# A graph network's gathers: GpSimd's rests wait for three tiles of a quad, with the fourth on a semaphore of its own

## The chip, the cores and the metric

The kernel runs on one core of one Trainium2 chip. The metric is the device time of one execution in microseconds: the median of the runs shown.

## The reference

Four graph networks follow each other on 3125 nodes of 128 features and 50000 edges that are sorted by their destination. After each, its output is added to its input and the sum is normalised over the features. What matters here is that every layer gathers a row of a node table for every edge, by the edge's source, and adds the results up by destination:

```python
def _layer(h, src, dst, e_w, w_neigh, w_root, b_root, g, b):      # network 0, three layers
    msg = e_w[:, None] * h[src]
    agg = jax.ops.segment_sum(msg, dst, num_segments=N)
    sum_w = jnp.clip(jax.ops.segment_sum(e_w, dst, num_segments=N), 1.0, None)
    out = agg / sum_w[:, None]
    out = out @ w_neigh.T + h @ w_root.T + b_root
    ...
# network 1: an edge network on edge_attr, joined with x[row], one layer
combined = jnp.concatenate([x[row], ef], axis=1)
msg = jax.nn.relu(combined @ Wn1 + bn1) @ Wn2 + bn2
out = jax.ops.segment_sum(msg, col, num_segments=x.shape[0])
# network 2: two layers with a table row for each source and edge type (8 types)
msg = xt[src, etypes]
agg = jax.ops.segment_sum(msg, dst, num_segments=x.shape[0])
# network 3: two attention layers; keys and values gathered by source and edge type (32 types)
kw = kT[src, :, etype]
m = vT[src, :, etype]
a = jnp.einsum('ehd,ehd->eh', kw, q[dst]) * pri[:, etype].T / SQRT_D
att = edge_softmax(a, dst, n)
```

## The kernel before

**Tiles, quads and steps.** The edges stand in 391 tiles of 128 (`EDGE_TILES`), four tiles to a quad, 98 quads (`TILE_QUADS`), the last with three tiles. A block of 128 nodes gets its sum by matmuls of a one-hot matrix (edge by node in the block) with the gathered rows, added up in PSUM. A tile whose edges reach over the end of a block is used twice, so the consumers go through 416 steps, 104 step quads, and look up in tables (`slot_i`, `blk_i`, `need_i`) which tile, which block and how many quads a step needs.

**Eight gather passes.** In each, `gathers` (L466) issues on GpSimd one indirect DMA for each tile (L479). It fetches 128 rows by the indices in `idx_s` into a ring of 60 tiles (`RING`) in SBUF. The passes, in order of time: 1 to 3 are the layers of network 0 (`aggregate_phase`, L683), of which 2 and 3 are the edge passes, in which `EdgeShare` also computes half of network 1's edge network on TensorE, ScalarE and VectorE and stores it; 4 is the block at L1182, which adds the stored edge part (`joins`); 5 and 6 are `aggregate_phase` for network 2; 7 and 8 are `score_phase` (L1874) of network 3, whose rows are 256 wide and in which SyncE also stores four tiles of values a step quad. Between the passes stand phases on the nodes, and every pass ends with a barrier of all engines.

**What orders the gathers.** The order is written out by hand. Four gathers of a quad go to one of 16 semaphores, `gathered[k % 16]`, 16 counts each. `hand_over(k)` (L470) waits for 64 counts more on that semaphore and raises `arrived` by one. VectorE waits for `arrived` in `release_steps` (L542) and passes `step_ready` on to TensorE; in pass 4 VectorE and in passes 7 and 8 VectorE and SyncE wait for it directly. From tile 60 on, GpSimd waits before each quad in `freed` for the step quad that last used the slots (`quad_done`, in other passes `mixed`), counted for the worst place of the block borders: at tile 60 it asks for step 28, so 32 tiles are in between; later in a pass this grows.

**The rests.** After the fourth tile of a quad, the loop below L480 hands over all quads but the newest, so that GpSimd waits for nothing that is in flight. Only where the number of quads is a multiple of `rest` does it hand over the newest too, and so waits until the gather that it issued last has landed. This is a rest. `rest` is 2 in the edge passes and 4 in the others.

```python
if t % 4 == 3:
    done = t // 4 + 1
    for k in range(handed[0], done if done % rest == 0 else done - 1):
        hand_over(k)
        handed[0] = k + 1
```

In an edge pass nothing is left over between rests, so both quads are handed over at the rest. After the loop the last two quads are handed over.

Of the kernel before, what the change touches and what calls it, by code (L numbers as in the profile page):

```python
# [17 lines left out]
H = 128  # L18
# [6 lines left out]
U = 16  # L25
# [7 lines left out]
EDGE_TILES = -(-E // P)  # L33
# [63 lines left out]
def build(nc, A, out):  # L97
    ctx = ExitStack()
    with ctx:
        def sb(name, shape, dt=F32):  # L100
            return ctx.enter_context(nc.sbuf_tensor(name, shape, dt))

        def signal(name):
            return Signal(ctx.enter_context(nc.semaphore(name)))

        def dram(name, shape, dt=F32):
            return nc.dram_tensor(name, shape, dt, kind="Internal").ap()


        table = dram("table", [NP, H])  # L110
        table8 = dram("table8", [NP * R8, H])
        table32 = dram("table32", [TABLE_NODES * T32, 2 * H])
# [27 lines left out]
        idx_s = sb("idx_s", [P, STEPS], I32)  # L140
# [39 lines left out]
        fetched = signal("fetched")  # L180
        go = signal("go")
        gathered = [signal(f"gathered{u}") for u in range(U)]
        arrived = signal("arrived")
        onehot_ready = signal("onehot_ready")
        step_ready = signal("step_ready")
# [280 lines left out]
        def gathers(pool, tab, width, freed, joins=None, rest=4):  # L466

            handed = [0]

            def hand_over(k):  # L470

                pool.wait_ge(gathered[k % U].sem, gathered[k % U].at(64 * (k // U) + 16 * min(4, EDGE_TILES - 4 * k)))
                if joins is not None:
                    joins(pool, k)
                pool.sem_inc(arrived.sem, 1)
            for t in range(EDGE_TILES):
                if t % 4 == 0 and t >= RING:
                    freed(pool, (t - RING + 3 + NB - 1) // 4)
                pool.indirect_dma_start(ring[:, ds(t % RING * 2 * H, width)], None, tab,  # L479
                                        bass.IndirectOffsetOnAxis(ap=idx_s[:, t:t + 1], axis=0)).then_inc(gathered[t // 4 % U].sem, 16)  # L480
                if t % 4 == 3:
                    done = t // 4 + 1
                    for k in range(handed[0], done if done % rest == 0 else done - 1):
                        hand_over(k)
                        handed[0] = k + 1
            for k in range(handed[0], TILE_QUADS):
                hand_over(k)

# [60 lines left out]
        def quad_pass_over():  # L549
            onehot_ready.base += ALL_QUADS  # L550
            quad_done.base += ALL_QUADS

        def gather_pass_over():
            quad_pass_over()
            arrived.base += TILE_QUADS
            for k in range(TILE_QUADS):
                gathered[k % U].base += 16 * min(4, EDGE_TILES - 4 * k)

        def fill_rows(pe, row):

# [122 lines left out]
        def aggregate_phase(tab, weight, root=None, row=None, sums=None, edges=None, ahead=None):  # L683


            with nc.Block() as block:
                @block.gpsimd
                def _(pool):
                    if ahead:
                        ahead.gpsimd(pool)  # L690

                    def freed(pool, n):
                        pool.wait_ge(quad_done.sem, quad_done.at(n + 1))
                    gathers(pool, tab, H, freed, rest=2 if edges else 4)

                @block.vector
                def _(dve):
# [80 lines left out]
                if edges:  # L778
# [5 lines left out]
                    def _(act):  # L784
                        edges.activations(act)
            gather_pass_over()
            step_ready.base += ALL_QUADS
            if sums:
# [389 lines left out]
        if STAGE >= 2:  # L1178
# [3 lines left out]
            with nc.Block() as block:  # L1182
                @block.gpsimd
                def _(pool):
                    def freed(pool, n):
                        pool.wait_ge(mixed.sem, mixed.at(n + 1))

                    def joins(pool, k):
                        pool.wait_ge(ring_in[k % HALF].sem, ring_in[k % HALF].at(16 * (k // HALF + 1)))
                    gathers(pool, table, H, freed, joins, rest=4)  # L1190

                @block.sync
                def _(sp):
# [43 lines left out]
                def _(pe):  # L1237
# [21 lines left out]
                    trips(pe, body)  # L1259
                    add_totals(pe)  # L1260
            gather_pass_over()
            totals_over()
            mixed.base += ALL_QUADS
# [340 lines left out]
        if STAGE >= 4:  # L1604
# [269 lines left out]
            def score_phase():  # L1874
# [4 lines left out]
                with nc.Block() as block:  # L1879
                    @block.gpsimd  # L1880
                    def _(pool):
                        stored_quads = [-1]

                        def freed(pool, n):
                            pool.wait_ge(mixed.sem, mixed.at(n + 1))
                            for m in range(stored_quads[0] + 1, n + 1):
                                pool.wait_ge(ring_out[m % QUADS].sem, ring_out[m % QUADS].at(64 * (m // QUADS + 1)))
                            stored_quads[0] = n
                        gathers(pool, table32, 2 * H, freed, rest=4)

                    @block.sync
                    def _(sp):
# [77 lines left out]
                onehot_ready.base += ALL_QUADS  # L1970
                arrived.base += TILE_QUADS
                for q in range(TILE_QUADS):
                    gathered[q % U].base += 16 * min(4, EDGE_TILES - 4 * q)
                for s in row_in:
                    s.base += 16 * TRIPS
                for s in (mixed, made, copied):
# [181 lines left out]
            for l in range(2):  # L2158
# [44 lines left out]
                by_type_phase(None, kvq_weights[l], sorted_kvq, layer=l)  # L2203
                key_value_table_phase(columns=l == 0)
                score_phase()
                softmax_phase()
                message_phase()
# [187 lines left out]
```

## Time and profile before

| | |
|---|---|
| median of 3 runs | 6471.04 us (6457.61 to 6473.24) |
| the profiled execution, its own time | 6410.16 us |
| its span | 6408.1 us |
| GpSimd busy | 3221.9 us (50%), of it the 3128 gathers 3001.8 us |
| TensorE busy, matmuls | 3293.9 us (51%) |
| VectorE, ScalarE busy | 2162.9 us (34%), 1006.4 us (16%) |

A share of busy time is an average over all stages. A gather on GpSimd is busy while its descriptors are written; the transfer lands later and isn't seen as busy time. A gap on GpSimd is shown in brackets ahead of the instruction that ended it, with what released it where the profile can tell; "issue" says only that it can't.

### The profile page before, as it was taken

The page shows a single profiled execution, that of the slowest core. Times are in us where ns is not written, and L with a number is a line of the kernel's source. Part 1 is how long each engine was busy: PE and PEld are TensorE (multiplying, and loading weights), DVE is VectorE, ACT ScalarE, POOL GpSimd, SP SyncE. Part 2 cuts the span into 40 slices and gives each one's busy share as a digit, 9 for nine tenths or more (in the row PEclk, how much of TensorE's full clock was granted, in tenths as well). Part 3 has the DMA queues.
Part 4 walks back from the last instruction along what each step waited for, and adds up shares of the span by engine and source line. Part 5 has one row for each costly group of instructions (what it writes and reads, how often), then busy time and mean ns, then how long its engine had stood idle before and what let it go on. Part 6 is the DMA issues. An engine that isn't in the chain of part 4 may idle for free. (4 is left out here: it accounts for less than half of the span.)

```text
span 6408.1 us, 51881 instructions
## 1 busy us (share of the span) xinstructions
PE 3293.9 (51%) x13857; PEld 2295.6 (36%) x13857; DVE 2162.9 (34%) x5075; ACT 1006.4 (16%) x2209; POOL 3221.9 (50%) x3406
## 2 busy tenths in 40 slices
PE   5554677767774555643463344643324356333263
PEld 3333455545552333332343232233324322333153
DVE  3222322232224222411121114533338544333485
ACT  0000322232222111200010002400004324000063
POOL 4665466546663666366646663046650320566403
PEclk7676777677776777755565556755557677555586
DMA  2111334333432332211131116976653579766453
GB/s 61 46 47 40 88 98 101 98 82 99 101 99 79 91 90 82 107 46 47 46 131 47 46 46 251 427 239 185 182 149 111 149 287 427 204 187 184 118 148 95
DMA packets 630965, 826.34 MB, mean 129 GB/s; under 512 B 93075, under 2 KB 510341, under 8 KB 618133
## 3 DMA queue, kind: packets, MB, share of 16 engines
q1 hardware_dynamic: 480117, 492.37, 22.9%
q0 software_dynamic: 120608, 276.12, 16.2%
q10 hardware_dynamic: 29952, 54.54, 2.9%
q8 instruction: 116, 1.90, 0.1%
q14 instruction: 172, 1.41, 0.1%
HBM read 470.63 MB, written 352.04 MB: 128 GB/s over the span
## 5 line engine op out<-in xcount | busy, mean ns | idle before, releaser
L479 POOL DMA_INDIRECT arena<-table,idx_s x3128 | 3001.8, 960 | 2353.5 <-issue 1095.5
L751 PE MATMUL ps<-arena,work 128*128 x4160 | 985.9, 378 | 1050.0 <-issue 934.9
L751 PEld LDWEIGHTS ps<-arena,work 128*128 128x128 f32 x4160 | 824.8, 274 | 1317.4 <-issue 1170.3
L1965 PE MATMUL ps<-arena,work 128*128 x1664 | 412.7, 426 | 693.7 <-issue 488.2
L1965 PEld LDWEIGHTS ps<-arena,work 128*128 128x128 f32 x1664 | 359.1, 317 | 748.6 <-issue 530.1
L459 DVE TENSOR_SCALAR work<-iota_row,dl_s,w_s 128x128 f32<-128x128 f32 x1248 | 350.4, 358 | 454.6 <-issue 349.4
L455 DVE TENSOR_TENSOR work<-ps,dl_s 128x512 f32<-128x512 f32 x208 | 143.8, 692 | 926.5 <-issue 617.0
L1934 DVE TENSOR_TENSOR arena<-arena,ps 128x128 f32<-128x128 f32 x832 | 182.7, 281 | 741.9 <-issue 500.0
L929 DVE SCALAR_TENSOR_TENSOR arena<-ps,vecs,arena 128x256 f32<-128x256 f32 x208 | 100.6, 484 | 893.9 <-issue 435.9
L1832 PE MATMUL ps<-arena,work 32*128 32x512 f32 x1600 | 299.1, 876 | 97.5 <-DVE work L1859 44.2
L510 PE MATMUL ps<-work,picks 128*104 128x512 f32 x416 | 313.4, 842 | 46.2 <-issue 42.8
L1863 DVE COPY arena<-ps 128x1024 f32<-128x1024 f32 x200 | 238.6, 1221 | 271.0 <-DMA table<-arena 164.8
L1254 PE MATMUL ps<-work,arena 128*128 128x128 f32 x832 | 173.5, 373 | 248.6 <-ACT arena L1232 153.7
L1654 POOL DMA_INDIRECT sorted_x<-work,pos_i x50 | 48.6, 973 | 479.8 <-DVE work L1747 465.2
L1254 PEld LDWEIGHTS ps<-work,arena 128*128 128x128 f32 x832 | 148.4, 267 | 382.4 <-ACT arena L1232 231.5
L863 PE MATMUL ps<-arena 128*128 128x128 f32 x832 | 212.3, 400 | 83.9 <-DVE arena L929 41.7
L1850 ACT ACTIVATE arena<-ps 128x1024 f32<-128x1024 f32 x200 | 198.1, 1022 | 309.7 <-DMA table<-arena 187.0
L1216 DVE TENSOR_TENSOR arena<-arena 128x128 f32 x416 | 94.7, 288 | 414.3 <-issue 245.1
L2145 PE MATMUL ps<-arena,onehot 128*128 128x128 f32 x1664 | 209.4, 280 | 21.7 <-DVE arena L2125 17.0
L863 PEld LDWEIGHTS ps<-arena 128*128 128x128 f32 x832 | 164.8, 278 | 123.0 <-DVE arena L929 64.2
L857 PE MATMUL ps<-arena 128*128 128x256 f32 x416 | 193.3, 560 | 28.9 <-ACT arena L897 25.0
L2145 PEld LDWEIGHTS ps<-arena,onehot 128*128 128x128 f32 x1664 | 194.7, 191 | 36.2 <-issue 30.7
(331 smaller groups left out, 3539.5 us busy)
## 6 DMA issues: line engine op xcount, KB each, us to landing
table<-arena SPq DMA_DIRECT2D x96, 2048.0 KB
onehot<-col_rows ACTq DMA_DIRECT2D x208, 256.0 KB
values<-arena SPq DMA_DIRECT2D x832, 64.0 KB
arena<-values SPq DMA_DIRECT2D x208, 256.0 KB
arena<-table,idx_s POOLq DMA_INDIRECT x3128
arena<-edge_times SPq DMA_DIRECT2D x208, 128.0 KB
edge_part<-arena SPq DMA_DIRECT2D x208, 128.0 KB
table<-arena SPq DMA_DIRECT2D x50, 512.0 KB
```

Of the source, the lines that this page charges most:

```text
L459: is_dst = dve.tensor_scalar(home[:, at + c, :], iota, dl_s[:, ds(j + c, 1)], weight[:, ds(j + c, 1)], ALU.is_equal, ALU.mult)
L479: pool.indirect_dma_start(ring[:, ds(t % RING * 2 * H, width)], None, tab, bass.IndirectOffsetOnAxis(ap=idx_s[:, t:t + 1], axis=0)).then_i ...
L510: mm = pe.matmul(quad_sums, picks[:, ALL_QUADS - n:2 * ALL_QUADS - n], deep[:, 4 * (n % DEEP):4 * (n % DEEP) + 4, :].rearrange("p c e -> p ...
L751: mm = pe.matmul(accf[:, ds(b, P)], o, arena[:, ds(slot, H)], start=False, stop=False, skip_group_check=True)
L857: pe.matmul(self.half_b, self.We2, self.hid[:, r, :], start=True, stop=True, skip_group_check=True).then_inc(turned.sem, 1)
L863: mm = pe.matmul(self.half_a[:, c * P:(c + 1) * P], self.ef[:, r, c * P:(c + 1) * P], self.Wn1b, start=True, stop=True, skip_group_check=True)
L1254: mm = pe.matmul(accf[:, ds(b, P)], relu_h[:, (i * U + u) % (4 * RELUS), :], o, start=False, stop=False, skip_group_check=True)
L1832: mm = pe.matmul(ps[:, 4 * kv + g, :], (value_ring if kv else key_ring)[rows, b % 2, :], (pair_v if kv else pair_k)[rows, half * 16:(half ...
L1850: act.activation(rows32[:, m % 3, :, kv * H:kv * H + 64].rearrange("p t (g c) -> p g t c", g=2), ps[:, 4 * kv:4 * kv + 2, :].rearrange("p ...
L1863: dve.tensor_copy(rows32[:, m % 3, :, kv * H + 64:(kv + 1) * H].rearrange("p t (g c) -> p g t c", g=2), ps[:, 4 * kv + 2:4 * kv + 4, :].re ...
L1965: mm = pe.matmul(ps[:, n % 8, c * P:(c + 1) * P], across_ring[:, n % DEEP, c * P:(c + 1) * P], Qn_flat[:, ds(b, P)], start=True, stop=True)
L2145: mm = pe.matmul(accf[:, ds(b, P)], o, msgs[:, 4 * q + c, :], start=False, stop=False, skip_group_check=True)
```

## The change

Of each quad only the first three tiles count on `gathered[k % 16]`, 48 counts a quad; the fourth counts on a new semaphore `fourth[k % 16]`. `hand_over(k)` waits for both. After the fourth tile of quad k is issued, quad k - 1 is always handed over, and never quad k. A rest is now a wait for the 48 counts of quad k alone, so for its first three tiles, while the fourth is in flight, and it stands behind the hand-over of quad k - 1. `rest` becomes 1 in the edge passes and 2 in the others. The loop ends with k = 96, so an edge pass has 97 rests and another pass has 48. The sums of the semaphores after a pass are changed to match.

```diff
+        fourth = [signal(f"fourth{u}") for u in range(U)]
...
-                pool.wait_ge(gathered[k % U].sem, gathered[k % U].at(64 * (k // U) + 16 * min(4, EDGE_TILES - 4 * k)))
+                pool.wait_ge(gathered[k % U].sem, gathered[k % U].at(48 * (k // U) + 16 * min(3, EDGE_TILES - 4 * k)))
+                if 4 * k + 3 < EDGE_TILES:
+                    pool.wait_ge(fourth[k % U].sem, fourth[k % U].at(16 * (k // U) + 16))
...
-                                        bass.IndirectOffsetOnAxis(ap=idx_s[:, t:t + 1], axis=0)).then_inc(gathered[t // 4 % U].sem, 16)
+                                        bass.IndirectOffsetOnAxis(ap=idx_s[:, t:t + 1], axis=0)).then_inc((fourth if t % 4 == 3 else gathered)[t // 4 % U].sem, 16)
                 if t % 4 == 3:
-                    done = t // 4 + 1
-                    for k in range(handed[0], done if done % rest == 0 else done - 1):
-                        hand_over(k)
-                        handed[0] = k + 1
+                    k = t // 4
+                    if k > 0:
+                        hand_over(k - 1)
+                        handed[0] = k
+                    if (k + 1) % rest == 0:
+                        pool.wait_ge(gathered[k % U].sem, gathered[k % U].at(48 * (k // U) + 48))
...
-                    gathers(pool, tab, H, freed, rest=2 if edges else 4)
+                    gathers(pool, tab, H, freed, rest=1 if edges else 2)
...
-                    gathers(pool, table, H, freed, joins, rest=4)
+                    gathers(pool, table, H, freed, joins, rest=2)
...
-                        gathers(pool, table32, 2 * H, freed, rest=4)
+                        gathers(pool, table32, 2 * H, freed, rest=2)
```

GpSimd's instructions at the start of the first pass (`rest` 4, then 2), with the semaphores that each waits for. A number behind x is a run of gathers without a wait, and a wait stands in the row of the gather behind it. Before:

```order
L479 DMA arena<-table,idx_s 128x128 x8
L479 DMA arena<-table,idx_s 128x128 [waits gathered0]
L479 DMA arena<-table,idx_s 128x128 x3
L479 DMA arena<-table,idx_s 128x128 [waits gathered1]
L479 DMA arena<-table,idx_s 128x128 x3
L479 DMA arena<-table,idx_s 128x128 [waits gathered2,gathered3]
L479 DMA arena<-table,idx_s 128x128 x7
L479 DMA arena<-table,idx_s 128x128 [waits gathered4]
```

Now:

```order
L482 DMA arena<-table,idx_s 128x128 x8
L482 DMA arena<-table,idx_s 128x128 [waits gathered0,fourth0,gathered1]
L482 DMA arena<-table,idx_s 128x128 x3
L482 DMA arena<-table,idx_s 128x128 [waits gathered1,fourth1]
L482 DMA arena<-table,idx_s 128x128 x3
L482 DMA arena<-table,idx_s 128x128 [waits gathered2,fourth2,gathered3]
L482 DMA arena<-table,idx_s 128x128 x3
L482 DMA arena<-table,idx_s 128x128 [waits gathered3,fourth3]
```

Before, the row with gathered2 and gathered3 is the rest behind 16 gathers. Now the row with gathered1 behind 8 gathers, and the one with gathered3 behind 16, are rests that leave the fourth tile out.

GpSimd's instructions at the start of the second edge pass (`rest` 2, then 1). Before:

```order
L479 DMA arena<-table,idx_s 128x128 x8
L479 DMA arena<-table,idx_s 128x128 [waits gathered0,gathered1]
L479 DMA arena<-table,idx_s 128x128 x7
L479 DMA arena<-table,idx_s 128x128 [waits gathered2,gathered3]
L479 DMA arena<-table,idx_s 128x128 x7
```

Now:

```order
L482 DMA arena<-table,idx_s 128x128 x4
L482 DMA arena<-table,idx_s 128x128 [waits gathered0]
L482 DMA arena<-table,idx_s 128x128 x3
L482 DMA arena<-table,idx_s 128x128 [waits gathered0,fourth0,gathered1]
L482 DMA arena<-table,idx_s 128x128 x3
L482 DMA arena<-table,idx_s 128x128 [waits gathered1,fourth1,gathered2]
L482 DMA arena<-table,idx_s 128x128 x3
```

A wait stood behind every second quad; now one stands behind each, and what it hands over is the quad before. Nothing moves on the other engines.

## Rows read from the trace of the kernel before

**Rows 1.** The page: span, busy time of each engine, and the gathers' group.
```profile
span 6408.1 us, 51881 instructions
PE 3293.9 (51%) x13857; PEld 2295.6 (36%) x13857; DVE 2162.9 (34%) x5075; ACT 1006.4 (16%) x2209; POOL 3221.9 (50%) x3406
...
L479 POOL DMA_INDIRECT arena<-table,idx_s x3128 | 3001.8, 960 | 2353.5 <-issue 1095.5
```

**Rows 2.** Windows of the eight passes, line L479 alone.
```profile
core 0: us, POOL busy (x), PEclk, DMA share, GB/s
63.95:617.42 553.47, 370.21 (x391) 0.65 0.18 47
672.80:1271.96 599.16, 371.44 (x391) 0.71 0.39 99
...
2000.03:2566.79 566.76, 394.17 (x391) 0.72 0.32 91
2652.31:3211.35 559.04, 377.30 (x391) 0.55 0.18 46
3276.95:3829.38 552.43, 370.49 (x391) 0.54 0.19 51
4206.91:4778.12 571.21, 373.68 (x391) 0.52 0.65 183
5465.61:6037.76 572.15, 372.85 (x391) 0.52 0.66 184
sum 4574.11, POOL 3001.83; mean POOL 375.23
```

**Rows 3.** Timeline, GpSimd, pass 1: start, length, instruction, [idle before].
```profile
82.87 0.95 POOL L479 DMA_INDIRECT arena<-table,idx_s  x1 [0.30 <-issue]
86.22 0.95 POOL L479 DMA_INDIRECT arena<-table,idx_s  x1 [2.41 <-issue]
87.47 0.95 POOL L479 DMA_INDIRECT arena<-table,idx_s  x1 [0.30 <-issue]
```

**Rows 4.** Timeline of all engines around a rest of the first edge pass.
```profile
1002.79 0.95 POOL L479 DMA_INDIRECT arena<-table,idx_s  x1 [0.30 <-issue]
1004.88 0.47 ACT L908 ACTIVATE arena<-ps,vecs 128x256 f32<-128x256 f32 x1 [5.54 <-remote]
...
1005.38 0.48 DVE L929 SCALAR_TENSOR_TENSOR arena<-ps,vecs,arena 128x256 f32<-128x256 f32 x1 [6.21 <-issue]
...
1006.00 0.95 POOL L479 DMA_INDIRECT arena<-table,idx_s  x1 [2.27 <-DMA arena<-table,idx_s]
...
1006.94 1.06 PE L751 MATMUL ps<-arena,work 128*128 x4
...
1010.55 0.48 DVE L929 SCALAR_TENSOR_TENSOR arena<-ps,vecs,arena 128x256 f32<-128x256 f32 x1 [3.55 <-issue]
```

**Rows 5.** Timeline, GpSimd: a long edge rest, then score rests of passes 7 and 8.
```profile
771.38 0.95 POOL L479 DMA_INDIRECT arena<-table,idx_s  x1 [3.25 <-DMA arena<-table,idx_s]
...
4326.24 0.95 POOL L479 DMA_INDIRECT arena<-table,idx_s  x1 [4.48 <-DMA arena<-table,idx_s]
...
5534.70 0.95 POOL L479 DMA_INDIRECT arena<-table,idx_s  x1 [2.58 <-issue]
```

**Rows 6.** Timeline, GpSimd, first edge pass: a pause behind a rest.
```profile
1018.08 0.95 POOL L479 DMA_INDIRECT arena<-table,idx_s  x1 [2.37 <-issue]
1019.97 0.95 POOL L479 DMA_INDIRECT arena<-table,idx_s  x1 [0.94 <-issue]
```

**Rows 7.** Timeline, TensorE beside GpSimd: pass 1, its end, the end of pass 6.
```profile
145.71 0.37 PE L751 MATMUL ps<-arena,work 128*128 x1 [2.44 <-issue]
...
147.11 0.29 PEld L751 LDWEIGHTS ps<-arena,work 128*128 128x128 f32 x1 [2.52 <-issue]
...
148.50 0.37 PE L751 MATMUL ps<-arena,work 128*128 x1 [2.42 <-issue]
...
161.18 0.95 POOL L479 DMA_INDIRECT arena<-table,idx_s  x1 [0.30 <-issue]
...
165.34 1.00 PE L751 MATMUL ps<-arena,work 128*128 x3 [0.34 <-issue]
...
165.62 0.94 POOL L479 DMA_INDIRECT arena<-table,idx_s  x1 [3.49 <-remote]
...
620.08 1.45 PE L751 MATMUL ps<-arena,work 128*128 x6 [1.73 <-issue]
...
634.07 1.05 PE L751 MATMUL ps<-arena,work 128*128 x8
...
3831.71 0.37 PE L751 MATMUL ps<-arena,work 128*128 x1 [0.33 <-issue]
3832.43 6.82 PE L751 MATMUL ps<-arena,work 128*128 x42 [0.34 <-issue]
```

More of the change, by code:

```diff
@@ L556, in gather_pass_over @@
             for k in range(TILE_QUADS):
-                gathered[k % U].base += 16 * min(4, EDGE_TILES - 4 * k)
+                gathered[k % U].base += 16 * min(3, EDGE_TILES - 4 * k)
+                fourth[k % U].base += 16 * (4 * k + 3 < EDGE_TILES)
         def fill_rows(pe, row):
@@ L1972, in score_phase @@
                 for q in range(TILE_QUADS):
-                    gathered[q % U].base += 16 * min(4, EDGE_TILES - 4 * q)
+                    gathered[q % U].base += 16 * min(3, EDGE_TILES - 4 * q)
+                    fourth[q % U].base += 16 * (4 * q + 3 < EDGE_TILES)
                 for s in row_in:
```

## The prediction

> **What bounds the kernel now.** I read the page first, then the windows of the eight gather passes, then the timeline of GpSimd inside them, and last TensorE beside it.
>
> The page: one core, 6408.1 us, no engine over 51% busy [rows 1]. The group of gathers, L479, holds 3001.8 of GpSimd's 3221.9 us, and its idle time names mostly "issue", that is, nothing that the view can name. The windows [rows 2] tell more: eight stretches of 391 gathers each fill 4574 us of the 6408. In each, GpSimd is busy for some 370 us of 552 to 600; the rest is gaps. The timeline [rows 3] shows the two kinds. A plain gap between gathers is 0.30 us (a gather takes 0.95, so one starts every 1.25), and at a rest it is 2.35 to 2.41: GpSimd waits until the last gather it issued has landed. A rest therefore costs 2.39 - 0.30 = 2.09 us more than no rest. There are 24 in a pass with `rest=4` (a rest after 16 gathers) and 48 in an edge pass.
>
> Does GpSimd set each pass's end? Yes. In an edge pass the consumers stand idle before the rest ends: ScalarE after 5.54 us, VectorE after 6.21 [rows 4]. VectorE's two joins there (L929) start 5.17 us apart where data is ready, while GpSimd supplies a quad every 6.1 us. In the first pass TensorE ends 17.7 us after the last gather (634.07 + 1.05 - 617.42), the longest such end of the passes [rows 2, 7].
>
> **The change, part by part.** The extra time of all rests of a pass is its length less busy time less 390 plain gaps (390 x 0.30 = 117 us) [rows 2].
>
> *Passes 1, 5 and 6 (`rest` 4 to 2).* 24 rests at 2.09 cost 50.2 us. The new rest waits for the third tile. That was issued 1.25 us before the fourth, so if it takes as long to land, the wait ends 1.25 earlier: 2.09 - 1.25 = 0.84. There are 48 of them: 40.3. Gain 9.9 each, 30 together.
>
> *Pass 4 (L1182, `rest` 4 to 2).* 566.76 - 394.17 - 117 = 55.6; less 2 for pauses (below), over 24, is 2.23 a rest. Then 0.98 x 48 = 47.0 against 53.6: gain 7.
>
> *Edge passes 2 and 3 (`rest` 2 to 1).* 599.16 - 371.44 - 117 = 110.7; less 3.3 for pauses is 107.4, or 2.24 a rest. Then 0.99 x 97 = 96.0: gain 11 each, 23 together. The trace has no wait for a third tile, so this is bounded by the rests of this pass: the shortest (2.27) gives 2.27 - 0.30 - 1.25 = 0.72, or 70 us (gain 38); the 3.25 one would give 1.70, or 165 us (loss 57) [rows 4, 5]. I take the value from the mean, since most rests stand near it.
>
> *Score passes 7 and 8.* These gathers are twice as wide and go beside four stores a quad. 571.21 - 373.68 - 117 - 2 = 78.5, and 80.3 for the other: 3.31 a rest. The single gaps spread from 2.58 to 4.48 [rows 5]. By the mean the new rest costs 3.31 - 1.25 = 2.06, times 48 is 99, a loss of 20 each. By the shortest it costs 1.03, or 49, a gain of 30 each. I take 1.65, between them, because the quads' stores will start one quad at a time and no longer in twos; 1.65 x 48 = 79: no change. So here the trace says that landing late, not the count, makes the rest long. The Trainium skill ("DMA: Bandwidth & Descriptors", section "Anatomy of one DMA") gives a GpSimd DMA a fixed cost of about 2.0 us plus bytes over 436 GB/s. By that, 128 KB would land 0.15 us after 64 KB, a score rest would cost 2.24 like the others and the new one 0.99, an estimate from that page: 48 x 0.99 against 24 x 2.24, or 6 us gained each. The gaps of 4.48 us speak against it, and I go by the rows.
>
> *Pauses.* Behind some rests a second gap of 0.94 us follows one gather later [rows 6]: three times in a pass with `rest=4` and five in an edge pass. I count them as tied to rests: 5 in the six passes and 10 in the edge passes, 0.65 more each: 6 x 2 x 0.65 + 2 x 5 x 0.65 = 14 us lost. The bounds are 0 and double.
>
> *Later hand-over.* Each quad is handed over one quad later, behind the next four gathers; before, only the quads not at a rest were. In exchange the quads at a rest come 5 us later. VectorE, SyncE in the score passes and TensorE behind them wait for this count; the ring gives 32 tiles of slack at the start of a pass, so GpSimd's own wait for `quad_done` stays covered. If that cover went, each wait would cost as the 3.49 one in [rows 7]. The last two quads are handed over behind the last gather as before, and quad 95 comes before the last three gathers (3 x 1.25 us and the last one's landing, 5.8 us in all), enough for one quad of 5.17. Nil. The extra semaphores and waits lie in the 0.30 gaps, where waits on landed quads cost nothing today (the gap stays 0.30 at such places). Nil.
>
> Sum: -30 - 7 - 23 + 0 + 14 = -46 us. The profiled execution took 6410.2 us around a span of 6408.1; the median of the runs is 6471.0, 1% more. I carry the difference over: 6471 - 46 = **6425 us**.
>
> **Rivals.**
>
> *TensorE's slow stretches spread (slower).* In the first pass TensorE falls to one instruction every 1.40 us, weight load and matmul in turn, up to 165 us, while GpSimd issues [rows 7]. GpSimd then waits 3.49 us for it, and TensorE runs at full pace 3.2 us after GpSimd's last issue. Again at the end: gathers end at 617.42, full pace from 620.08. At the end of pass 6 it is the same: single matmuls to 3831.71, then 42 in a row [rows 7]. What frees TensorE seems to be some 3 us with no issue. The edge passes, with a rest every 10 us, show no such stretch (a stretch of one at its ordinary pace is in [rows 4]); rests of 1.3 us may be too short to prevent them. It decides if they appear in passes 2 and 3. Price: five stalls of 3.2 a pass, 16 us, and a backlog that does not shrink, since 5.2 us a quad hardly beats the supply of 6.0: eight quads left behind the last gather, 42 us. Twice 58 is 116, so 6471 - 46 + 116 = **6541**. Against it: those passes keep TensorE busy, and pass 4, with rests as rare as pass 1, shows no stretch either.
>
> *The stretches cease (faster still).* If it is the count of rests that matters, passes 1, 5 and 6 lose their stalls: 553.47 - 370.21 - 117 - 50.2 - 2 = 14 us, and 13 and 13 in the others. With 7 us of the first pass's end that is 47: **6378**.
>
> *The third tile is no earlier (no change).* With a quad released at each hand-over, the edge loads and stores meet every quad's gathers. If the rests of the edge and score passes then cost 10 us more a pass than I take, and the gain in passes 1, 4, 5 and 6 stays, it is -46 + 40: 6465, up to 6490 with the doubled pauses. For it: gaps of 3.25 and 4.48 exist. Against: most edge rests are near 2.4.
>
> *It does not do what it says.* The order of GpSimd's instructions shows the new waits where they should be; no chance of its own.
>
> **How the numbers follow.** My case has 43%, its own range 6395 to 6460; the stretches cease 14%; no earlier tile 17%; the stretches spread 26%. A measurement can tell 0.3%, 19 us, from no change. Faster: 0.37 of the first case and the 0.14, so 0.51. The same: 0.20, most of the third case and the weak end of the first. Slower: 0.29. The range takes in both outer cases: 6370 to 6550.
>
> **What would show it.** In the timeline of GpSimd, gaps of 1.1 to 1.2 us where 2.35 stood in passes 1, 5 and 6, 48 to a pass, and 97 of some 1.3 in the edge passes. In the windows, passes 1, 5 and 6 shorter by 10 us, the edge passes by 11, the score passes the same. The forecast is wrong if the edge passes grow, if TensorE shows instructions 1.40 us apart in them, or if the score rests stay over 2.4.

## The result and the profile after

The changed kernel took **6591.95 us** (median of 4 runs, 6586.73 to 6608.93) where the kernel before took 6464.32 (6445.94 to 6473.24): 1.0206 times as long, interval 1.0175 to 1.0236. Forecast were 6425, with a range of 6370 to 6550. The prediction was wrong in its direction, and the result lies outside its range.

The page of the changed kernel, against [rows 1]: 182 us more span, the same busy time of GpSimd, VectorE and ScalarE, and 186 us less on TensorE, whose ends are modelled by the profile.

```profile
span 6590.3 us, 52308 instructions
PE 3108.3 (47%) x13857; PEld 2171.2 (33%) x13857; DVE 2166.0 (33%) x5075; ACT 1006.5 (15%) x2209; POOL 3217.9 (49%) x3406
...
L482 POOL DMA_INDIRECT arena<-table,idx_s x3128 | 2996.5, 958 | 2442.5 <-issue 787.6
```

The eight gather passes as windows of L482 alone, against [rows 2].

```profile
62.37:618.41 556.04, 370.49 (x391) 0.65 0.18 46
677.59:1275.96 598.37, 370.94 (x391) 0.70 0.36 92
1372.20:1973.22 601.02, 371.04 (x391) 0.67 0.37 92
2084.74:2649.71 564.97, 387.13 (x391) 0.63 0.33 91
2754.86:3315.89 561.03, 377.53 (x391) 0.57 0.18 46
3379.91:3931.94 552.03, 371.23 (x391) 0.57 0.19 51
4311.81:4890.35 578.54, 374.26 (x391) 0.52 0.62 177
5603.72:6187.57 583.85, 373.87 (x391) 0.53 0.61 175
```

The lengths have hardly moved: 556.0 for 553.5 in pass 1, 598.4 for 599.2 in the first edge pass, 22 us more in all. The distances between the rows have: from the last gather of an edge pass to the first of the next pass it was 54.9 and 73.3 us (1326.9 - 1272.0 for the first) and is 96.2 (1372.20 - 1275.96) and 111.5. Behind pass 4 it was 85.5 and is 105.1. I call such a distance the tail of its pass; all eight tails together (the last one runs to the end of the span) are 162 us longer. With the 22, less the 1.6 us by which the first gather comes earlier, that makes the 182.

Is the short rest short? GpSimd in pass 1, columns as in [rows 3]:

```profile
83.14 0.95 POOL L482 DMA_INDIRECT arena<-table,idx_s  x1 [0.56 <-issue]
...
93.70 0.95 POOL L482 DMA_INDIRECT arena<-table,idx_s  x1 [0.86 <-DMA arena<-table,idx_s]
...
103.98 0.94 POOL L482 DMA_INDIRECT arena<-table,idx_s  x1 [0.58 <-DMA arena<-table,idx_s]
```

It is: 40 of the 48 gaps at rests in pass 1 are under 1 us, with a median of 0.60, so a rest costs 0.30 us more than a plain gap and not the 0.84 that I took. But the pass did not become shorter, because GpSimd now stands elsewhere. TensorE beside GpSimd in pass 1:

```profile
143.89 0.37 PE L757 MATMUL ps<-arena,work 128*128 x1 [2.43 <-issue]
...
145.29 0.37 PE L757 MATMUL ps<-arena,work 128*128 x1 [1.03 <-issue]
...
145.99 1.71 PE L757 MATMUL ps<-arena,work 128*128 x5 [0.33 <-issue]
...
147.08 0.95 POOL L482 DMA_INDIRECT arena<-table,idx_s  x1 [7.38 <-remote]
```

TensorE's slow stretch, in [rows 7] a matter of 3.49 us for GpSimd, makes it wait for 7.38, and TensorE returns to its full pace while GpSimd is silent. Of such gaps there are twelve in pass 1, of 3.1 to 7.4 us. What the rests gave up, these took.

The first edge pass has no such slow stretch. There, signals come late. All engines around a short rest, against [rows 4]:

```profile
1102.40 0.71 PE L869 MATMUL ps<-arena 128*128 128x128 f32 x4 [1.20 <-issue]
...
1104.34 0.95 POOL L482 DMA_INDIRECT arena<-table,idx_s  x1 [0.30 <-issue]
1107.09 0.38 ACT L903 ACTIVATE arena<-ps 128x256 f32<-128x256 f32 x1 [4.77 <-remote]
...
1107.89 0.95 POOL L482 DMA_INDIRECT arena<-table,idx_s  x1 [2.61 <-remote]
```

ScalarE's L903 reads what TensorE's L869 writes; the profile names L869 as the releaser of 33 other waits of L903 in this pass. L869 ended at 1103.11 and L903 starts at 1107.09, 4.0 us later. GpSimd waits at the same time and goes on 0.8 us after ScalarE; from 1105.29 to 1107.89 it issued nothing. The waits by line and releaser (total us, times, longest); the first two rows are the edge pass of the changed kernel, the third is its pass 4:

```profile
ACT arena L903 <- remote: 145.2, 23, 20.0
ACT arena L914 <- remote: 105.7, 19, 15.3
...
DVE work L456 <- remote: 164.5, 14, 25.2
```

and the same edge pass before, where the two lines are L908 and L897 and have one sixth of it:

```profile
ACT arena L908 <- remote: 28.5, 6, 5.5
...
ACT arena L897 <- remote: 12.7, 4, 3.3
```

"Remote" is a wait whose releaser the profile did not find. In pass 4 of the kernel before, the same line of VectorE (L455 there) has none.

### The profile page after: what moved, and what is told of

It reads as the page before. It is cut to its first block and busy times, and to the rows that moved or that the text cites. A ratio compares the mean times of both kernels' runs of the same rounds, so it can differ in the third digit from the quotient of the medians.

```text
span 6590.3 us, 52308 instructions
## 1 busy us (share of the span) xinstructions
PE 3108.3 (47%) x13857; PEld 2171.2 (33%) x13857; DVE 2166.0 (33%) x5075; ACT 1006.5 (15%) x2209; POOL 3217.9 (49%) x3406
## 5 line engine op out<-in xcount | busy, mean ns | idle before, releaser
L482 POOL DMA_INDIRECT arena<-table,idx_s x3128 | 2996.5, 958 | 2442.5 <-issue 787.6
L757 PE MATMUL ps<-arena,work 128*128 x4160 | 878.5, 343 | 918.6 <-issue 903.0
L757 PEld LDWEIGHTS ps<-arena,work 128*128 128x128 f32 x4160 | 743.6, 246 | 1143.3 <-issue 1129.8
L1971 PE MATMUL ps<-arena,work 128*128 x1664 | 411.4, 418 | 717.9 <-issue 571.5
L1971 PEld LDWEIGHTS ps<-arena,work 128*128 128x128 f32 x1664 | 354.5, 310 | 776.0 <-issue 617.5
L515 PE MATMUL ps<-work,picks 128*104 128x512 f32 x416 | 275.0, 735 | 97.4 <-issue 96.9
L869 PE MATMUL ps<-arena 128*128 128x128 f32 x832 | 195.1, 372 | 207.2 <-issue 138.8
L869 PEld LDWEIGHTS ps<-arena 128*128 128x128 f32 x832 | 145.6, 248 | 252.0 <-issue 161.8
```

The lines of the kernel that those rows point to most:

```text
L515: mm = pe.matmul(quad_sums, picks[:, ALL_QUADS - n:2 * ALL_QUADS - n], deep[:, 4 * (n % DEEP):4 * (n % DEEP) + 4, :].rearrange("p c e -> p ...
L757: mm = pe.matmul(accf[:, ds(b, P)], o, arena[:, ds(slot, H)], start=False, stop=False, skip_group_check=True)
L869: mm = pe.matmul(self.half_a[:, c * P:(c + 1) * P], self.ef[:, r, c * P:(c + 1) * P], self.Wn1b, start=True, stop=True, skip_group_check=True)
L1971: mm = pe.matmul(ps[:, n % 8, c * P:(c + 1) * P], across_ring[:, n % DEEP, c * P:(c + 1) * P], Qn_flat[:, ds(b, P)], start=True, stop=True)
```

## The experiments

**Theory A**: gathers in flight make the other engines' instructions and signals late. Only a rest in which everything lands lets them catch up; a short one is worth nothing, and the later hand-over is innocent. **Rivals**: the count of rests hurts; the later hand-over does; the silence of GpSimd counts, not what it waits for.

A comparison is a session in which some kernels and the kernel before ran beside each other. The comparisons came in two conditions, each of which held for all kernels of a comparison. The kernel before read 6462 to 6477 us in the first, third and fifth (and 6464 in the comparison of the result), and 6347 to 6352 in the second and fourth; the second and the third ran on one and the same chip. Ratios are always to the kernel before of the same comparison.

The traces tell the conditions apart as clearly as the times. As a slow stretch I count four or more starts on TensorE in a row that lie 1.3 to 1.5 us apart. Pass 1 has 7 to 15 of them in each trace of the first, third and fifth comparison, in that of the changed kernel and in that of the kernel before, and no pass has one in the eight traces of the second and fourth. The clock doesn't tell them apart: the runs of the kernel before had a mean granted clock of 0.648 to 0.653 in the second comparison and of 0.649 to 0.651 in the third.

### First comparison (before: 6462.33)

`e1_full_same`: full rests at the old places, with the new semaphores and the later hand-over kept.

```diff
+                        pool.wait_ge(fourth[k % U].sem, fourth[k % U].at(16 * (k // U) + 16))
-                    gathers(pool, tab, H, freed, rest=1 if edges else 2)
+                    gathers(pool, tab, H, freed, rest=2 if edges else 4)
```

and `rest=4` for 2 in pass 4 and the score passes.

> The changed kernel, but each rest also waits for the fourth tile, and rests stand where they stood before (every second quad in edge passes, every fourth elsewhere). Left of the change: the split semaphores and the hand-over one quad later. Theory A (short rests do not let the other engines catch up; the old rest, which ends when the last gather has landed, does): back at the time before, 6464 us within 20, and TensorE ends 10 to 12 us behind the last gather of an edge pass, not 50. Theory B (the later hand-over makes the consumers late): stays within 20 of the changed kernel's 6592.

Measured: 6475.16 us, ratio 1.0026 (1.0007 to 1.0046). The whole loss is gone, so the semaphores and the later hand-over cost 0.3%, and 0.5% at the upper end of the interval. Its windows of the first three passes:

```profile
63.07:621.40 558.33, 369.58 (x391) 0.64 0.18 46
674.23:1269.63 595.40, 370.51 (x391) 0.69 0.40 100
1322.88:1921.92 599.04, 370.45 (x391) 0.70 0.40 99
```

Its tails behind the edge passes are 53.2 (1322.88 - 1269.63) and 73.7, as before. Signals are still late at times: the remote waits of the same two lines of ScalarE are 106.5 us in the first edge pass, against 250.9 in the changed kernel.

`e2_three_same`: the short rest at the old places (the `rest=` edits of e1 without its first line).

> The changed kernel with its rests for three tiles, but at the places of before: 48 in an edge pass and 24 in the others. Theory A: a short rest is worth nothing, so half of them cost half: the same as the changed kernel or up to 40 us less in issue time, with the tails behind the edge passes still 40 to 50 us; 6550 to 6600. Rival (the short rests do help, and there must be many): clearly slower than 6592, by 30 us or more. Rival (there are too many rests now): near 6464 less 40.

Measured: 6611.54 us, 1.0222 (1.0178 to 1.0267). This is 11 us above the range that I had given; the count of the rests is innocent too.

`e3_no_rest`: no rest anywhere.

```diff
-                    if (k + 1) % rest == 0:
-                        pool.wait_ge(gathered[k % U].sem, gathered[k % U].at(48 * (k // U) + 48))
```

> The changed kernel without any rest; each quad is handed over one quad later as in it. Theory A: GpSimd's own gaps at rests go, but it waits as long for the engines behind it, so within 40 us of the changed kernel's 6592, tails of 40 us and more. If short rests are worth something: above 6640.

Measured: 6582.6 us, 1.0179 (1.0136 to 1.0221): a short rest is worth as much as none. Its first two passes:

```profile
63.63:615.32 551.69, 369.38 (x391) 0.65 0.18 47
679.04:1265.30 586.26, 369.74 (x391) 0.71 0.38 94
```

Without a rest, pass 1 still takes 551.69 us, though 391 gathers with plain gaps would need 369.4 + 117 = 486. TensorE sets this pass, with its slow stretches and its late counts, and not GpSimd.

`e4_edges_full`: full rests of the old spacing in the edge passes alone, the changed kernel elsewhere.

```diff
+                        if rest_full:
+                            pool.wait_ge(fourth[k % U].sem, fourth[k % U].at(16 * (k // U) + 16))
-                    gathers(pool, tab, H, freed, rest=1 if edges else 2)
+                    gathers(pool, tab, H, freed, rest=2, rest_full=bool(edges))
```

> The changed kernel, but the edge passes have their old rests back (every second quad, until the fourth tile has landed). Theory A: the two edge passes lose their tails, 2 x 40 us, the other passes stay as changed: 6592 - 80 = 6512 within 20. Theory B: stays at 6592.

Measured: 6508.39 us, 1.0066 (1.0046 to 1.0086). The edge passes hold about two thirds of the loss of 2.1%; their tails are 52.0 and 70.1, and that behind pass 4 is 110.5.

### Second comparison (before: 6351.89)

`e5_busy_2us` and `e6_busy_1us`: no wait for a landing; GpSimd is kept busy by memsets instead, at the old places (three in e5, two in e6).

```diff
-                        pool.wait_ge(gathered[k % U].sem, gathered[k % U].at(48 * (k // U) + 48))
+                        for r in range(3):
+                            pool.memset(idle[:, 0:600], 0.0).then_inc(paused.sem, 1)
+                            paused.base += 1
+                            pool.wait_ge(paused.sem, paused.base)
```

> The kernel of e1_full_same, but at a rest GpSimd waits for no gather: it fills 600 columns of a scratch tile three times instead, each after the one before, some 2.1 us without a gather being issued. If it is the time without a new gather that lets the other engines catch up, this is as good as e1_full_same, 6475 within 25, with edge tails of 10 to 15 us. If GpSimd has to be quite idle, it is like e3_no_rest: 6580 within 25.

> The same with two fills, some 1.4 us in which no gather is issued, about the time at which the last one lands. If any pause of this length will do, as e5_busy_2us or a few tens of us less. If a pause must last past the landing (the old rest ends 0.8 us behind it), near 6580.

Measured: e5 6211.63 us, 0.9783 (0.9767 to 0.9799); e6 6061.0 us, 0.9542 (0.9526 to 0.9558). Both are far below all that was expected, and below the kernel before. From the end of one gather to the start of the next, the pause takes 2.19 us in e5 and 1.54 in e6, and a full rest 2.37 (medians of pass 1 in the traces).

`e7_full_denser` and `e8_full_sparser`: full rests at every third quad of an edge pass and every second elsewhere (e7), at every fourth and every eighth (e8). The edit is that of e1 with other numbers.

> The kernel of e1_full_same with full rests at other places: every third quad in edge passes, every second elsewhere. Read pass by pass. Edge passes: 16 rests fewer save up to 34 us a pass in gaps, if the tails stay at 11; if three quads are too far apart, tails grow to 30 and more. Passes 1, 4, 5, 6: 24 rests more at 2.09 are +50 us each if GpSimd has no other wait to give up for them, less where it waits for TensorE today. Score passes: the stores that stand behind the last gather (some 30 us of the tail) may go.

> The same with rests at every fourth quad in edge passes and every eighth elsewhere. Theory A: edge tails near those of the changed kernel (45 us), with gaps no smaller, since GpSimd waits for the ring instead. Passes 1, 5, 6: if their rests are worth nothing, as long as now; if they are, the end behind the last gather grows by 5 to 15 us.

Measured: e7 6585.39 us, 1.0373 (1.0356 to 1.0391); e8 6034.25 us, 0.9505 (0.9489 to 0.9521). e7's passes are what rests as a pure cost make of them: pass 1 takes 589.2 us and the first edge pass 561.9. e8 missed what was expected of it: fewer rests were faster by far, and no tail grew. Its first two passes:

```profile
62.48:576.17 513.69, 369.75 (x391) 0.68 0.20 50
622.16:1168.30 546.14, 369.98 (x391) 0.77 0.44 109
```

Pass 1 has the 12 full rests that `rest=8` gives, and takes 513.69: the gathers and plain gaps, 369.75 + 117, and 27 us for them, 2.2 each. Here GpSimd alone sets the pass, and TensorE shows no slow stretch anywhere in this trace; nor has the edge pass a remote wait. The tail behind the first edge pass is 51.3.

### Third comparison (before: 6476.97)

Was it the kernels or the conditions? The changed kernel, e3, e6 and e8 were run again, unaltered. (The expectations count 490 short and 242 full rests; by the loops it is 482 and 240, and the differences in rests that they divide by are 120 for e8 and 112 for e7, not 122 and 116.)

> The changed kernel once more, beside the kernel before of the same chip. The four runs of the second comparison (before at 6351.89 there against 6462.33 in the first) had short tails behind every pass of gathers, and there a full rest cost 2.0 to 2.6 us each: (6351.89 - 6034.25) / 122 rests fewer and (6585.39 - 6351.89) / 116 rests more. Theory A (two conditions of the chip: where TensorE keeps up, rests are pure cost; where it does not, a full rest is what lets it): if before reads near 6350 here, the changed kernel pays 490 short rests of 0.9 for 242 full ones of 2.3, so about 6235, with tails behind the edge passes near 52; if before reads near 6460, it repeats its 1.02, near 6590, with tails near 96. Theory B (the short rest is bad on every chip, and the second comparison differed by its kernels alone): 1.02 in both cases, tails near 96.

> The changed kernel with all its rests left out, again. Theory A: where before reads near 6350, 242 full rests of 2.3 are gone and nothing takes their place: 5730 to 5850. Where before reads near 6460: 6583 as in the first comparison (ratio 1.018). Theory B: 1.018 in both cases, since gathers that are not held back keep TensorE late.

> The memset pause (1.35 us extra at the old places, no wait for any landing), again. Theory A: where before reads near 6350, 6061 again. Where before reads near 6460, the pause does not hold the gathers until their data has landed, so it works as the short rest did: 6550 to 6620. Theory B (what matters is how long GpSimd issues nothing, not for what it waits): 6060 to 6200 in both cases.

> Full rests at every fourth quad in the edge passes and at every eighth in the others, again. Theory A: where before reads near 6350, 6034 again. Where before reads near 6460, half of the full rests leaves half of the help: 6480 to 6580, tails behind the edge passes of 60 to 90. Theory B (a full rest is what counts, few are enough): 6030 to 6150 in both cases.

Measured: e9 6618.84 us, 1.0214 (1.0196 to 1.0233); e10 6596.11, 1.0181 (1.0162 to 1.02); e11 6637.8, 1.0244 (1.0224 to 1.0264); e12 6651.57, 1.0261 (1.0241 to 1.0282). The pause of e11 is 577 us slower than the same kernel was as e6, e12 617 us slower than as e8. Where before is near 6470, the pause is no better than a short rest. Half of the full rests is even worse than none (1.0261 against 1.0181). Both lie above the ranges that I had given. The same two passes as above, in e12:

```profile
62.75:621.64 558.89, 369.96 (x391) 0.65 0.18 46
674.75:1287.97 613.22, 369.48 (x391) 0.66 0.35 91
```

Same gathers, same busy time, 45 and 67 us more, and a tail of 95.3 behind the edge pass, which is that of the changed kernel, though each of its 24 rests waits until everything has landed.

### Fourth comparison (before: 6346.95)

`e13_denser_again` is e7. `e14_agg_none` has the full rests of before in the edge passes, pass 4 and the score passes, and none in passes 1, 5 and 6:

```diff
-                    gathers(pool, tab, H, freed, rest=1 if edges else 2)
+                    gathers(pool, tab, H, freed, rest=2 if edges else 1000000)
```

`e15_edges_each` has a full rest at every quad of the edge passes (`rest=1 if edges else 4`). `e16_full_and_pause` has a full rest and two of e5's memsets behind it.

> Full rests at every third quad in the edge passes and every second in the others (358 in place of 242). Where before reads near 6350: 6585 again (2.0 us for each of 116 rests more). Where before reads near 6460 to 6480 (late signals): Theory A (each full rest lets the late signals through): edge passes get fewer rests and longer tails (52 to about 70 each), the others twice as many, whose length is no longer bought back: 6560 to 6660.

> Full rests as before in the edge passes, pass 4 and the score passes, none in passes 1, 5 and 6. Where signals are late, these three passes were 553 to 559 us long with full rests, with short ones and without any, and their tails 55 to 70: TensorE holds them. Theory A: rests are bought back there to the last us, so without them 6460 to 6500, the same as before within 0.5%. Where signals are not late (before near 6350): 72 rests of 2.3 less, about 6190. Rival: the backlog of pass 1 is carried on and the edge tails grow: 6520 and more.

> A full rest at every quad of the edge passes (98 more), the others as before. Where signals are late: Theory A says that the tails behind the edge passes, 55 and 73 in before, are already those of a pass without backlog (the four runs of the second comparison had 52 and 71), so that nothing is left to win: 98 rests of 1.7 to 2.6 add 165 to 250, less what TensorE held up anyway (6 to 10 us a pass): 6600 to 6700. Rival: a rest takes its place inside a wait that is there anyway and costs 1 us or less: 6480 to 6560.

> Full rests at the old places, each followed by the memset pause of 1.35 us. Theory A (the pause itself is dead time, once the landing has been waited for): 242 x 1.35 = 327 us more where signals are not late (near 6680), and 200 to 330 more where they are (6670 to 6800). Theory B (the length of the silence is what counts, and 2 us are too short to clear TensorE's slow stretches in passes 1, 5 and 6): the slow stretches cease, worth up to 40 us in each of six passes: 6430 to 6600.

Measured: e13 6587.43 us, 1.0383 (1.0365 to 1.04); e14 6164.72, 0.9715 (0.9699 to 0.9731); e15 6549.78, 1.0318 (1.0301 to 1.0335); e16 6532.01, 1.0296 (1.0278 to 1.0313). In this condition every rest is a cost: e15's 98 more cost (6549.78 - 6346.95)/98 = 2.07 each. Pass 1 of e15 and of e16:

```profile
62.84:602.26 539.42, 369.47 (x391) 0.70 0.19 48
```

```profile
61.88:622.38 560.50, 369.91 (x391) 0.69 0.18 46
```

With its 24 full rests e15's takes 539.42, e14's with none 488.59: 2.12 a rest. e16's pause adds 21.1/24 = 0.88 a rest, not 1.35, so its time came out below what I had written for it. It lies in the range of Theory B there, but not for B's reason: this condition has no slow stretches that could cease. Neither e15 nor e16 met the other condition.

### Fifth comparison (before: 6462.31)

> The changed kernel beside before, a third time. If before reads near 6350 (tails of 45 to 53 behind the passes): Theory A (rests are pure cost there) has its 490 short rests at 0.9 (441 us) take the place of 242 full ones at 2.3 (557 us): 6200 to 6270, ratio 0.98 to 0.985. Theory B (the change is bad whatever the condition): 1.02, 6480. If before reads near 6465 to 6480: 1.02 by both, near 6600.

> Full rests in the edge passes, pass 4 and the score passes only, again. If before reads near 6350: 6165 as in the comparison before this one. If before reads near 6465 to 6480: Theory A (TensorE holds passes 1, 5 and 6 at 553 to 559 whatever GpSimd does): within 0.5% of before; rival (the backlog is carried on): 6520 and more.

Measured: e17, the changed kernel, 6600.06 us, 1.0212 (1.0164 to 1.0259). e18, which is e14, 6469.39 us, 1.0013 (0.9996 to 1.0031). Theory A's forecast for it held: where TensorE holds the pass, the rests of passes 1, 5 and 6 are worth nothing, and without them no more than some 8 us are carried on into the edge passes. But its pass 4 has two slow stretches and a tail of 91.9 us with all of its 24 full rests, where e1 has no stretch and 83.8.

The same kernel in the two conditions, windows of the first two passes (and of the first score pass, pass 7, for e14) and the waits of pass 1. e14:

```profile
63.84:552.43 488.59, 369.76 (x391) 0.72 0.21 53
599.29:1198.87 599.58, 369.70 (x391) 0.71 0.40 99
...
3989.16:4551.15 561.99, 371.49 (x391) 0.52 0.68 187
```

```profile
DVE work L460 <- POOLq L478: 371.6, 97, 6.2
PEld ps L758 <- DVEq L553: 267.7, 95, 3.6
```

e18:

```profile
62.13:617.11 554.98, 369.43 (x391) 0.66 0.16 46
673.08:1266.97 593.89, 370.31 (x391) 0.69 0.38 99
```

```profile
PEld ps L758 <- issue: 319.6, 294, 3.5
...
DVE work L460 <- remote: 99.7, 14, 11.9
DVE work L460 <- PE ps L758: 60.5, 9, 16.6
```

In e14 VectorE waits 97 times for GpSimd's count, once for nearly each quad, and TensorE waits for VectorE (DVEq and POOLq are the two engines' queues): a chain that GpSimd feeds. In e18 TensorE "waits" 294 times for nothing that the profile names, and VectorE and GpSimd wait for TensorE. The edge passes, with a full rest every second quad, are nearly the same in both, and the tail behind the first is 53.2 us in e14 and 61.1 in e18.

## Why the prediction was wrong

*What bounds the kernel.* I wrote that GpSimd sets each pass's end. For the edge passes with full rests that is right. For passes 1, 5 and 6 it was wrong: they take 550 to 564 us with full rests, short ones, pauses or none (e1, e2, e11, e3), while GpSimd alone needs 488.59 (e14). I had seen TensorE's slow stretches, and had booked them as 13 to 14 us a pass on top of the rests. They were the limit of these passes, and the rests merely used up time that was spent anyway.

*Passes 1, 5 and 6, gain 30.* Measured +2.6, +2.0 and -0.4: nothing. The cost of a short rest was even over-stated (0.84 for 0.30), but its gain went into GpSimd's waits for TensorE.

*Edge passes, gain 23.* The passes' lengths moved by -0.8 and +1.1 us. Rests of 0.64 (median gap 0.94) in place of 2.24 saved time at the rests and lost it at waits for late counts. Then came what I had priced at nothing in my own case: tails longer by 41.3 and 38.2.

*Pauses, loss 14.* Wrong in direction, and small. In the trace of before, 31 gaps of 0.5 to 1.05 us away from rests hold 19 us above the plain gap; in the changed kernel there are 9, with less than 5 us.

*Pass 4, gain 7.* Length -1.8, tail +19.6. I had used pass 4 as evidence against the rival, since it showed no slow stretch with rests as rare as pass 1. It got eight slow stretches, and VectorE's 164.5 us of remote waits, once its rests no longer waited for all.

*Score passes, nil.* +7.3 and +11.7 in length, +25.9 and +32.4 in tails. Yet the tails of these passes are as long in e1 (718.6 and 402.1 us; in the changed kernel 713.4 and 402.7), which is no slower than before. So they seem to be no effect of the change but what sets the profiled execution of before, 6410 us, apart from its median, 6464. The traces show where these tails grow. SyncE's stores of values fall behind during the pass, and the pass can't end before they are issued. Of the 416 stores of a score pass, 8 are left behind the last gather in every trace of the second and fourth comparison, 20 and 8 in that of before, and 44 to 60 in all others. In pass 7 of the changed kernel and of e8:

```profile
4893.40 36.55 SPq L1909 DMA_DIRECT2D values<-arena  x52
```

```profile
4453.59 4.62 SPq L1910 DMA_DIRECT2D values<-arena  x8
```

Full rests at the old spacing don't prevent this (e1 has 56), so SyncE is held up too.

As to the rule that I had weighed there: the Trainium skill ("DMA: Bandwidth & Descriptors", section "Anatomy of one DMA") would have a gather of 128 KB land 0.15 us after one of 64 KB. In e14, where no signal is late, a full rest of the score pass costs (561.99 - 371.49 - 118.8)/24 = 3.0 us, with four stores a quad beside the gathers and with 118.8 for the plain gaps as in its pass 1 (488.59 - 369.76). One of 64 KB gathers costs 2.1 (e15, pass 1). It was right to go by the rows.

*Later hand-over and semaphores, nil.* Nearly right: e1 costs 0.3% with both.

*The third tile lands 1.25 us before the fourth.* Right in its direction; the rest was even shorter than the sum had it.

*The rival.* "TensorE's slow stretches spread" had the right thought, that the short rest may be too short for the engines behind GpSimd to catch up, but not the mechanism of the edge passes. By its own words it is decided by whether the stretches appear in passes 2 and 3, and none of the 20 traces has one there. They appeared in pass 4 (none in before and e1, 8 now), which it did not name; in pass 1 they are as many without the change (7 in before, 13 in e1, 11 now). The edge passes were held by late signals instead. So it is luck that its backlog of eight quads, 42 us for each edge pass, is so near to the 41 and 38 us by which the tails grew. Against e1, the changed kernel is 114.5 us longer in the profiles (6590.3 - 6475.8), of which the tails of both edge passes and of pass 4 hold 43 + 38 + 21 = 102. I gave this rival 26% and 6541 us. It kept my gain of 46 us, which did not exist because the gain stood on the same waits.

**The step that failed** is the one that took a rest for a pure cost in GpSimd's time, and priced the shorter one by GpSimd's gap alone. In the condition of these runs a full rest at every second quad of an edge pass bought something that the view of GpSimd does not show: 2 us in which the others caught up. Its price was put at the gap, 2.24 us, and the tails that it saves at nothing; the runs showed that without it (e2, e3, and the changed kernel) the tails behind each edge pass are 38 to 43 us longer than in e1.

**What stays open.** Why a comparison comes in the one condition or in the other is not settled. It is not the gathers' transfers that are slower. Their queue on the pages of e8 and e12 (packets, MB, share of 16 engines):

```profile
q0 software_dynamic: 120608, 276.12, 17.9%
```

```profile
q0 software_dynamic: 120608, 276.12, 15.9%
```

Of 6024 and 6651 us that is 1078 and 1058. That the signals are late because gathers are in flight is inferred from their timing, and from the effect of full rests; the path on which the signals wait was not seen.

Nor is it settled what it is about the full rest that helps: that all has landed, or how long GpSimd stays silent. In e11's pauses the last packet of the gather before ended some 1.25 us after GpSimd was done with it, and the next gather came 1.54 us or more after, so nearly always all had landed there as well, and it did not help. In pass 1 the silence behind the last packet is 0.3 us in e11 and 1.1 in e1 (medians), and GpSimd fills the one pause with memsets and is idle in the other. Length alone doesn't settle it either: in e11's first edge pass 29 of the 48 gaps are over 2.3 us, since GpSimd waits there besides, and the tail is 96.1 us. A pause of e5's length from the start of a pass was not run in this condition. Nor is waiting for the landing enough by itself: e12 does it at every fourth quad and has the long tails, and e1's pass 1 still has 13 slow stretches.

The changed kernel met only the condition in which it loses, in three comparisons out of three. In the other, a short rest at the cost measured in pass 1 (0.30, against 2.12) would save 24 x 2.12 - 48 x 0.30 = 36 us in that pass. So it might well be faster there, which is an estimate and was not measured.

**The better version.** e14 (and e18) is the only one of the three kernels measured in both conditions that gained in one, 2.8%, and lost nothing in the other. e8 gains 5.0% and loses 2.6%.

## What to carry to other kernels

A wait on the engine that feeds all others is not only a cost: before it is shortened, ask what the others do during it. If they catch up exactly there, it is their time, and the backlog that a shorter one leaves comes due behind the last transfer, where nothing covers it. To learn which engine sets a pass, remove its waits altogether in one run: pass 1, at 551.69 us without a rest against 553.47 with 24, would have answered the question at once. And a tuning that rests on such an effect has to be measured in more than one session, since the same kernel came out at 0.954 and at 1.024 of the one beside it.

## What the runs showed of the hardware

- In the gather passes TensorE can fall to an instruction each 1.40 us (11 stretches in pass 1 of the changed kernel), ScalarE can start 4.0 us after the matmul that it needs, and SyncE can have 52 stores left behind the last gather of a score pass, against 8. This is a condition of the session and not of the kernel. It was there in the comparison of the result and in three of the five since, and absent in two; one chip had both.
- Where it is absent, the cost of rests is exact arithmetic: pass 1 takes 488.59, 513.69 and 539.42 us with 0, 12 and 24 full rests, 2.1 for each.
- Where it is present, a pause of GpSimd that does not wait for landings (e11, 1.0244) did not take the full rest's place (e1, 1.0026). Its gap between gathers is 1.54 us and that of the full rest 2.37; whether a pause of that length would do was not tried in this condition.
